# A graph network on one core: the last slot of each of six walks in another order, a constant added on VectorE, a norm in place

## What is computed

```python
def reference(x, src, dst, edge_attr_128, edge_weight, ...):
    h = jnp.maximum(_layernorm(x), 0.0)
    x = x + L0(h)      # three weighted gcn layers (hops 0 to 2 of the kernel), then @ Wl + bl
    h = jnp.maximum(_layernorm(x), 0.0)
    x = x + L1(h)      # m = h[src] + edge_attr; mean per destination (hop 3); two @ with batch norms
    h = jnp.maximum(_layernorm(x), 0.0)
    x = x + L2(h)      # six times: agg = segment_sum(x[row], col); x = x + relu(agg / deg @ W.T + b)
    h = jnp.maximum(_layernorm(x), 0.0)
    x = x + L3(h)      # one gcn layer, tanh, @ W2 + b2
    return x
```

## Time and profile before

| | us |
|---|---|
| three runs | 3167.26, 3171.38, 3177.81 |
| median | 3171.38 |
| profiled execution | 3173.83 |
| its span | 3172.1 |

### The profile page before, as it was taken

The page is one execution under the profiler, slowest core; times in us unless marked ns, Lnnn a source line. Parts: engine busy times, 40 slices in busy tenths (PEclk is TensorE's granted clock), DMA queues, the critical chain, the costliest instruction groups (busy, mean ns, idle before and its releaser), DMA issues. The chain is left out here.

```text
span 3172.1 us, 46018 instructions
## 1 busy us (share of the span) xinstructions
PE 2513.3 (79%) x11251; PEld 1548.1 (49%) x11251; DVE 2030.2 (64%) x7784; ACT 1971.6 (62%) x4381; POOL 1440.7 (45%) x1507
## 2 busy tenths in 40 slices
PE   5787677787767788999999647899999999766840
PEld 2454444555555564444544323456565656444520
DVE  6655677788897662333333467787787878876620
ACT  1687777876777654555555478777767677755300
POOL 6666666365542640000000000567676766654576
PEclk8899888899877998999999758999999999977865
DMA  5666555455665653443334488665565656433311
GB/s 100 182 197 184 170 153 150 145 169 158 193 192 163 196 172 106 139 136 136 132 138 135 141 258 300 206 184 181 179 192 184 191 179 187 134 101 115 93 55 41
DMA packets 528965, 504.91 MB, mean 159 GB/s; under 512 B 58706, under 2 KB 389955, under 8 KB 528616
## 3 DMA queue, kind: packets, MB, share of 16 engines
q1 hardware_dynamic: 477388, 415.73, 40.8%
q0 software_dynamic: 47184, 85.73, 10.6%
q10 hardware_dynamic: 4172, 0.99, 0.2%
HBM read 246.45 MB, written 260.27 MB: 160 GB/s over the span
## 5 line engine op out<-in xcount | busy, mean ns | idle before, releaser
L1850 POOL DMA_INDIRECT h_G<-step_tab,row_i x294 | 286.8, 976 | 352.5 <-DMA step_tab<-l_NR 192.9
L800 PE MATMUL a_PA<-a_H,w 128*128 128x512 f32 x504 | 274.3, 674 | 89.4 <-ACT a_H L964 86.0
L1850 POOL DMA_INDIRECT h_M<-step_tab,row_i x294 | 285.2, 970 | 120.9 <-issue 86.6
L1563 DVE TENSOR_SCALAR b_Y<-b_BP,col 128x512 f32<-128x512 f32 x148 | 109.9, 742 | 354.4 <-PE b_BP L1517 354.4
L1545 ACT ACTIVATE b_Z<-b_BQ,bn 128x512 f32<-128x512 f32 x148 | 115.0, 777 | 257.3 <-PE b_BQ L1509 257.0
L1605 POOL TENSOR_TENSOR b_d<-b_d,neghalf 128x1 f32<-128x1 f32 x1 | 0.6, 565 | 592.2 <-DVE b_d L1596 592.2
L1517 PE MATMUL b_BP<-b_Z,w 128*128 128x512 f32 x592 | 266.3, 592 | 0.0
L270 POOL DMA_INDIRECT h_G<-msg_tab,row_i x147 | 143.0, 973 | 207.4 <-issue 111.4
L2217 DVE TENSOR_TENSOR_SCAN h_T<-keep,h_T,h_P 128x512 f32<-128x512 bf16 x196 | 222.9, 1137 | 12.2 <-PE h_P L1968 3.1
L239 ACT ACTIVATE a_HI<-a_X,a_ln_nm,a_ln_rs 128x128 f32<-128x128 f32 x490 | 201.0, 484 | 24.4 <-DVE a_ln_nm L222 24.4
L973 ACT ACTIVATE a_H<-a_PA,col 128x512 f32<-128x512 f32 x252 | 162.2, 668 | 82.7 <-PE a_PA L800 82.4
(11 more groups left out here) (385 smaller groups left out, 6452.3 us busy)
## 6 DMA issues: line engine op xcount, KB each, us to landing
b_HI<-hin_tab SPq DMA_DIRECT2D x148, 256.0 KB, 2.8
y_tab<-b_Y SPq DMA_DIRECT2D x148, 256.0 KB, 2.0
l_Y<-y_tab SPq DMA_DIRECT2D x148, 256.0 KB, 3.5
l_X<-x_tab SPq DMA_DIRECT2D x148, 256.0 KB, 4.5
x_tab<-a_X SPq DMA_DIRECT2D x112, 256.0 KB
hin_tab<-a_HI SPq DMA_DIRECT2D x112, 256.0 KB, 3.6
a_XR<-in_x SPq DMA_DIRECT2D x97, 256.0 KB, 4.3
out_rows<-l_O SPq DMA_DIRECT2D x97, 256.0 KB, 3.1
```

The lines of the kernel that those rows point to most:

```text
L800: nc.tensor.matmul(PA[b][:, 0:nt * P], w[:, :], h[b][:, 0:nt, :].rearrange("p t d -> p (t d)"), start=True, stop=True).then_inc(done, 1)
L1563: nc.vector.tensor_scalar(Y[b][:, :], BP[b][:, :], col[:, C_B12:C_B12 + 1], None, ALU.add).then_inc(b_y, 1)
L1850: pool.indirect_dma_start(out=GR_[i % 2][b][:, k, :], out_offset=None, in_=table[:, :], in_offset=bass.IndirectOffsetOnAxis(ap=row_i[:, t ...
```

## The change

Three things are changed.

1. In a walk's last slot (`ends_walk`) PE's x3 of the slot's pair stands behind the second iteration's blocks and products, and DVE's order becomes: sums of the second iteration, the late pair's output, affines and update, and only then statistics and rstd2 of the slot's pair. In the sixth walk that slot has no pair; there `end_rstd` moves behind `update`.
2. `rows_const` is gone. The copy of the result from PSUM into O becomes an addition of `rb32`, a tile with b2 on all partitions, loaded once by ACT's queue.
3. `m_apply` writes the norm in place, RS into RS, and waits for the x_tab store of these rows (m_x1_st). `m_store` stores RS. `m_scaled` is gone; the messages of hop 3 multiply RS by vscale while they add it, tile by tile, ahead of the wait for the features, and add the features last.

```diff
             if self.kind == "mean":
+                dve.wait_ge(mn.normed, 2 * i + b + 1)
+                for j in range(nt):
+                    last = nc.vector.scalar_tensor_tensor(rows[:, j, :], RS[:, t + j, :], vscale[:, t + j:t + j + 1], rows[:, j, :],
+                                                          ALU.mult, ALU.add)
+                last.then_inc(h_mid, 1)
+                dve.wait_ge(h_mid, 2 * i + b + 1)
                 dve.wait_ge(features_in[b], 16 * (i + 1))
-                nc.vector.tensor_tensor(rows[:, 0:nt, :], rows[:, 0:nt, :], features[b][:, 0:nt, :], ALU.add).then_inc(h_mid, 1)
-                dve.wait_ge(h_mid, 2 * i + b + 1)
-                dve.wait_ge(m_v, 2 * i + b + 1)
-                last = nc.vector.tensor_tensor(rows[:, 0:nt, :], rows[:, 0:nt, :], RS[:, t:t + nt, :], ALU.add)
+                last = nc.vector.tensor_tensor(rows[:, 0:nt, :], rows[:, 0:nt, :], features[b][:, 0:nt, :], ALU.add)
...
-                    sp.dma_start(edge_rows(msg_tab[3], RR, first_tile(i, b), nt), HR[b][:, 0:nt, :]).then_inc(m_h_st[b], 16)
+                    t = first_tile(i, b)
+                    sp.dma_start(edge_rows(msg_tab[3], RR, t, nt), RS[:, t:t + nt, :]).then_inc(m_h_st[b], 16)
...
             def m_apply(i):
                 for b in range(2):
                     t = first_tile(i, b)
-                    after(act, m_v, 2 * (i - 1) + b + 1)
-                    after(act, m_h_st[b], 16 * i)
-                    mn.act_apply(act, i, b, _Rows(RS, t), HR[b])
-
-            def m_scaled(i):
-                for b, nt in enumerate(SUB):
-                    t = first_tile(i, b)
                     act.wait_ge(m_x1_st[2 * (i % 2) + b], 16 * (i // 2 + 1))
-                    act.wait_ge(mn.normed, 2 * i + b + 1)
-                    for k in range(nt):
-                        last = nc.scalar.activation(RS[:, t + k, :], HR[b][:, k, :], AF.Copy, scale=vscale[:, t + k:t + k + 1])
-                    last.then_inc(m_v, 1)
+                    mn.act_apply(act, i, b, _Rows(RS, t), _Rows(RS, t))
...
-                    if hop.h == 2 and i > 1:
-                        m_scaled(i - 2)
...
                 if k == GAP[3]:
-                    m_scaled(IT - 2)
                     m_apply(IT - 1)
-                    m_scaled(IT - 1)
...
+    def ends_walk(its):
+
+        return bool(its) and its[-1] < F0 and (its[-1] + 1) % IT == 0
...
-                if late is not None:
-                    rows_const(late)
...
-                if j is not None and is_d(j):
+                if j is not None and is_d(j) and not ends_walk(its):
                     x3(j)
                 for i in its[1:]:
                     if i < F0:
                         hop_blocks(i, (0,))
                     hop_prod(i)
+                if j is not None and is_d(j) and ends_walk(its):
+                    x3(j)
...
-                    nc.vector.tensor_copy(O[b][:, :, :].rearrange("p t d -> p (t d)"), XB[r][b][:, :]).then_inc(o_set, 1)
+                    nc.vector.tensor_tensor(O[b][:, :, :], XB[r][b][:, :].rearrange("p (t d) -> p t d", d=D),
+                                            rb32[:, :].unsqueeze(1).broadcast_to([P, 4, D]), ALU.add).then_inc(o_set, 1)
...
-                if late is not None:
+                if late is not None and not ends_walk(its):
                     rows_out(late)
...
                 for i in its[1:]:
                     sums(i)
+                if ends_walk(its):
+                    if late is not None:
+                        rows_out(late)
+                    for b in range(2):
+                        affine(its[1], b)
+                    update(its[1])
                 if j is not None and is_d(j):
                     stats2(j)
```

More of the change, by code:

```diff
@@ L143, in build @@
     rbh = sb(top, "rbh", [P, D])
+    rb32 = sb(top, "rb32", [P, D])
     split_x1 = sb(top, "split_x1", [3, 512], BF16)
@@ L455, in build @@
     sp_f, sp_r = (XDW[1][0:1, b, :, :] for b in range(2))
-    HR, MH, FE = SN[0], R1, R2
+    MH, FE = R1, R2
     PA, P3 = [ps(ctx, f"a_PA{b}") for b in range(2)], [ps(ctx, f"a_P3{b}") for b in range(2)]
@@ L489, in build @@
                                                   sems("r2_st", 2))
-    xd_got, xd_st, xd_ld, wd_set, m_x1_st, m_h_st, m_v = ([sems(f"xd_got{k}", 2) for k in range(2)], [sems(f"xd_st{k}", 2) for k in range(2)], sems("xd_ld", 4),
-                                                                 sem("wd_set"), sems("m_x1_st", 4), sems("m_h_st", 2),
-                                                                 sem("m_v"))
+    xd_got, xd_st, xd_ld, wd_set, m_x1_st, m_h_st = ([sems(f"xd_got{k}", 2) for k in range(2)], [sems(f"xd_st{k}", 2) for k in range(2)], sems("xd_ld", 4),
+                                                            sem("wd_set"), sems("m_x1_st", 4), sems("m_h_st", 2))
     feat_in, feat_pad, mh_st, mh_ones = sems("feat_in", 2), sem("feat_pad"), sems("mh_st", 2), sem("mh_ones")
@@ L496, in build @@
     REST = E - FULL * P
-    N_LOADS = 29
+    N_LOADS = 30
     padded = [(t, base) for t in (hin_tab, x1_tab) for base in (E0, S0)]
@@ L915, in _ @@
                      (rbl[:, :], b0l.partition_broadcast(P)), (rbh[:, :], bh.partition_broadcast(P)),
+                     (rb32[:, :], b32.partition_broadcast(P)),
                      (w01[:, :], W01[:, :]), (w02[:, :], W02[:, :]),
@@ L1943, in prod @@
                     nc.tensor.matmul(PC[b][:, :], w31[:, :], HT[b][:, :, :].rearrange("p t d -> p (t d)"), start=True, stop=True).then_inc(p1_set, 1)
-            def rows_const(j):
-                for b in range(2):
-                    nc.tensor.matmul(XB[j % 2][b][:, :], ones3[:, :], split_out[:, :], start=False, stop=False, skip_group_check=True)
             def rows(j):
@@ L1954, in rows @@
                     for k in range(4):
-                        last = nc.tensor.matmul(XB[j % 2][b][:, k * P:(k + 1) * P], HT[b][:, k, :], w32[:, :], start=False, stop=(k == 3), skip_group_check=True)
+                        last = nc.tensor.matmul(XB[j % 2][b][:, k * P:(k + 1) * P], HT[b][:, k, :], w32[:, :], start=False, stop=True, skip_group_check=True)
                     last.then_inc(p2_set, 1)
@@ L2308, in _ @@
                 for i in its[1:]:
-                    if i < F0:
+                    if ends_walk(its):
+                        pass
+                    elif i < F0:
                         affine(i, 0)
@@ L2317, in _ @@
                 for i in its[1:]:
-                    if i < F0:
+                    if i < F0 and not ends_walk(its):
                         affine(i, 1)
```

## The result

The changed kernel took 3159.65 us (median of 17 runs), the kernel before 3177.52 beside it (17 runs): a ratio of 0.9954, 95% interval 0.9939 to 0.9968, so 14.6 us less (10.2 to 19.4); the two medians lie 17.9 apart. The forecast was 16.6 less. The profiled execution's span went from 3172.1 to 3155.1 us, at a granted clock of 0.894 instead of 0.892.

The account below looks back on a forecast made before the run. POOL's 98 gathers plus a boundary were taken to set each walk, with TensorE almost as tight. Boundaries -11.0, sixth walk +0.5, ahead of hop 3 -4.1, hop 3 -2.0: 3171.4 - 16.6 = 3154.8, forecast 3155 us, range 3143 to 3169.

Parts of the forecast that it names:

- The sum: Whole kernel: -11.0 + 0.5 - 4.1 - 2.0 = -16.6 us.
- 6.1 forecast for the norm: Third hop's norm in place: -4.1 us ahead of hop 3 and -2.0 in hop 3.
- The boundary, -11.0: Five boundaries between walks: shorter chain from last gather to last store saves 2.2 us each, -11.0 (-8 to -13.5).
- rival (a): Walk boundaries: out_rows stores queued ahead of step_tab's take gain back, 0.6 us a boundary, sum -8.6, 3162.8 us; chance 0.12.
- The output constant, 0 in the walks: TensorE loses 98 matmuls, 0.44 us a slot; POOL sets the walk, so only margin comes of it: 0.
- 1.9 us of room: Next walk's first turn ends at 2291.9, POOL needs its buffer at its 15th gather, 2293.8: 1.9 us of margin.
- rival (b): Walks: pushed-back pair makes the turn late, POOL waits at its 15th gather; 0 of the 11, 3165.8 us; chance 0.12.
- rival (d): Walks: TensorE's clock falls behind longer waits, half a slot costs 8.6 us; +16, 3188 us; chance 0.06.
- The sixth walk, +0.5: Sixth walk's last slot has no pair; only the statistics' reciprocal moves behind the update: +0.5 us.
- Ahead of hop 3, -4.1: Ahead of hop 3: two ScalarE scaling passes go, TensorE's 5.46 us wait for a_H shrinks: -4.1 us.
- -2.05 as the lower bound: Ahead of hop 3: if POOL's first gather leads, only the first scaling pass counts, gain 2.05 us.
- Hop 3, -2: Hop 3: 0.4 us less a slot behind the features' landing, -2 (-4 to +3), despite +10.5 us VectorE work.

Follow-up runs that it names:

- walk slot alone: Only the new order in a walk's last slot, against the kernel before: ratios 1.0024 and 1.0015 at 3596 us and above, 1.0030 at 3178 us.
- constant alone: Only the output constant moved into VectorE's addition, against the kernel before: ratios 0.9969 (beside 3655.77 us) and 0.9996 (beside 3177.49 us).
- the four profiles: Kernel before, constant alone, walk slot alone and whole change, all at 3178 us: sixth walk 191.62, 188.33, 197.52 and 193.38 us.
- norm alone: Only the third hop's norm in place, against the kernel before: ratios 0.9962 (beside 3655.77 us) and 0.9996 (beside 3596.34 us).

## Why the prediction was right, and where it was not

**The sum** of -16.6 stands against -14.6 (10.2 to 19.4). That it fits is in part luck. The walks gave 12.2 where 11 were forecast, but by a condition that the forecast had put at nothing (below). Of the 6.1 forecast for the norm the profile shows 2.9, and the last pass, forecast at 0, shows 6.1.

**The boundary, -11.0.** The mechanism and the size of the chain were right: 8.4 us to 6.33, 2.1 a boundary against 2.2. The five stillnesses fell by 14.8 in sum, of which 10.4 are that chain; of the rest 2.0 are earlier turns (3.55 behind the gather at the first boundary before) and 2.4 the restart (5.5 us from store to gather at the fourth before, 3.9 at the others). The gathers inside the walks took 2.7 us more in sum. POOL's restart followed the store by 3.7 to 3.9 us, with the out_rows stores issued from 2267.22 and the step_tab ones at 2269.48: rival (a) didn't happen in the whole change. By the Trainium skill (DMA: Bandwidth & Descriptors, "Queues, rings and completion order") the out_rows writes would have been in that wait; they were not to be seen in it. The distance doesn't explain that: from the end of the last out_rows issue to the step_tab issue it is 1.3 us at four boundaries and 0.2 at the second (restart 3.83), and ahead of hop 3, counted in the same way, a distance of 1.3 went with a wait of 4.84 us instead of 4.04.

**The output constant, 0 in the walks.** This is the step that was wrong, and it was wrong in its reasoning, not in its row. I wrote that nothing comes of TensorE's relief "but margin", since POOL sets the walk. Alone it brought nothing, 0.3 us. But the order alone brought a loss of 9.5 us, and only both together brought the gain. I had compared the pushed-back pair with one event, POOL's 15th gather, and found 1.9 us of room there. No wait came at that gather, but the room was smaller: the pair was late by 3.1 us by my own rows (2272.8 against 2269.74) and not 2.8, the first turn came 15.4 to 16.1 us behind POOL's start and not 15.1, and some 0.5 us were left (turn ended at 2153.0, gather at 2153.54). What I had not done is follow the lateness to the end of the walk, where it comes out in the last turn: TensorE is some 4 to 6 us later against POOL after a boundary of the new order, and a walk in which it gains 0.6 us a slot is too short to make that up; one in which it gains 1.1 is long enough. The difference is near the 0.44 us a slot that I had worked out for the constant and called idle. Seven slots of 0.44 are 3.1 us, and the last turn's lateness fell from 4.41 to 1.86. The margin pays for the order. At 3596 us and above the walk slot alone shows what rival (b) describes, waits of POOL for turns inside the walks.

**The clock, rival (d).** I had read 0.99 as the clock at the boundaries. It was an average over a whole walk and hid falls that were there already: over the 16 us from 1 us ahead of POOL's start it was 0.89, 1.00, 0.89, 0.96 and 1.00 at the five boundaries before, and 0.89 at one of five with the constant alone. The 11.8 us of the first boundary, from which I worked out a margin near nothing, hold such a fall; where none stands ahead of it the first turn comes at 8.6 to 10.2. With the new order the fall is more frequent, at nine of ten boundaries in two profiles (0.89, once 0.68) against four of ten, and some 3 us earlier: 0.79 of full over the first 8 us (0.69 once), so for part of them at the 1.2 GHz level. In the changed kernel TensorE waited 1.52 and 0.74 us for the pair's norm ahead of the fall, where it had waited 0.5. But at its second boundary it waited 1.59 and 0.74 us and kept 1.00, so these waits alone don't decide it. The price was small: four matmuls at 3.31 instead of 1.98 us, and the first turn 15.9 to 16.1 instead of 15.4 us behind POOL's start. I had priced half a slot, 8.6 us. The Trainium skill (TensorE: Matmul & The Clock Gate, "HAM oscillation — how this bites in real kernels") says that waits between groups of matmuls let the clock fall; the trace agrees that falls come behind waits, at some 1 us a boundary here, with the same waits once without a fall.

**The sixth walk, +0.5.** It grew by 1.8 in the whole change: in the four profiles by 5.1 to 5.9 with the order, less 3.3 to 4.1 with the constant. I had forecast 0.5 for the first and 0 for the second. That this walk isn't set by POOL, so that a pair pushed back is paid for at once and a shorter TensorE counts, is my reading of these four and not shown. In the last pass the slots did follow the constant (26.0 against 23.5 to 24.0 us).

**Ahead of hop 3, -4.1.** a_H came 4.1 us sooner as worked out, and the matmuls took 1.4 less at a higher clock. Then the lead passed to the gather, which I had put at -2.05 as the lower bound; it came 0.8 to 1.7 sooner. The stage gained 2.5 to 3.2 at 3178 us (3.4 to 4.4 above). I took the row of the engine that waits longest, and not the slower of the two chains.

**Hop 3, -2.** The wait for the features fell from 27.8 to 23.2 us in sum, in seven waits instead of six, but the stage only by 0.4, and the three profiles of the old norm at this level differ by 0.8 among themselves (164.0 to 164.8). No gain is shown, and none of the 10.5 us of added VectorE work was lost either, which the range allowed.

The first 1012 us came out 2.7 us longer in the changed kernel's profile; three other profiles at these conditions have the first gather of hop 1 at 628.5 to 629.9, the changed kernel has 633.7. The constant alone and the walk slot alone don't show it, the norm alone wasn't run at this level, and it stays open.

## What to carry to other kernels

Work that is pushed behind a deadline must be followed not to the next event that needs it but to the next deadline of the same kind: in a loop with one bound engine, the second engine's lateness can be carried through to the loop's end, as it was here, and only its slack summed over the loop pays it back. So test a reordering together with the relief that feeds it, and each alone, before one of them is called worthless: here one part alone was nothing, the other a loss, both together the gain. When a wait is cut, look for the transfer whose issue moves up against another's in the same queue; here a store was issued 2.1 us sooner, and the gather behind it started only 1.2 us sooner. And before a mean of the clock is taken for its value at a place, read short windows on both sides of it: 8 us showed 1.00 where the next 8 held the fall.

## What was not expected of the hardware

The granted clock fell behind waits as short as 1.5 and 0.7 us in a row, in a kernel whose walks run at 0.99 otherwise, and was back at 1.00 for 2142.9 to 2150.9; in the kernel before it fell behind waits of 0.5 and 1.3 us, and behind the same waits it also stayed at 1.00. The gather that reads a 448 KB pair of stores to HBM started 4.04 us after their issue with 2.6 us between it and the issue of the stores ahead, 4.84 with 1.3 us and 5.87 with none, while at the walks' boundaries a distance of 1.3 us went with 3.7 to 3.9 us in one kernel and mostly 4.4 to 4.6 in another.
